# One end of a fused attention and expert layer: pad transfers asked for earlier, one weight copy given to a transfer, router and ranks one step forward

## What is computed

```
x  = x + tanh(g_attn) * attention(layernorm(x), ctx)      # causal, 16 heads, keys and values from ctx
y  = layernorm(x)
e  = argmax(softmax(y @ Wr + br))                          # one expert per token
out = sum over all experts i of  relu((y if e == i else 0) @ W1[i] + b1[i]) @ W2[i] + b2[i]
x  = x + tanh(g_ffn) * out
```

## Time and profile before

| what | value |
|---|---|
| time of the profiled execution | 349.75 us |
| its span (first to last instruction) | 347.8 us, 1.95 us less |
| median of 3 runs | 350.26 us, 0.51 us above the profiled one |
| PE busy | 335.7 us, 97% of the span |
| DVE, ACT, POOL busy | 285.8 us, 247.9 us, 197.5 us |
| TensorE clock granted | 0.997 of full speed |
| last batch begins | about 261.8 us |
| first expert tile | 294.3 us |
| tile 7 transposed | 310.25 us |
| last product ends | 341.8 us |

### The profile page before, as it was taken

One profiled execution on the slowest core, in us unless ns is written; L12 is line 12 of the kernel. 1 busy time (PEld: TensorE's weight loads), 2 busy tenths in 40 slices (PEclk: granted clock), 3 DMA queues, 4 the chain that ended last, 5 costly groups with the idle time before them and its releaser, 6 DMA issues.

```text
span 347.8 us, 10938 instructions
## 1 busy us (share of the span) xinstructions
PE 335.7 (97%) x2827; PEld 282.3 (81%) x2827; DVE 285.8 (82%) x1288; ACT 247.9 (71%) x908; POOL 197.5 (57%) x401
## 2 busy tenths in 40 slices
PE   7999999999999999999999999999999999989993
PEld 6777878887987788879887988798888767979992
DVE  4778997798889888898889878988998896877871
ACT  3687776588758875887588758876887666757671
POOL 7243755367636763766376637653867553157553
PEclk9999999999999999999999999999999999999998
DMA  6999022000300030003000300040001944434320
GB/s 201 249 357 296 7 94 96 4 2 1 126 0 0 0 125 0 0 0 125 0 0 0 125 0 0 0 140 0 0 0 76 401 180 129 125 97 116 115 67 13
DMA packets 22618, 28.39 MB, mean 82 GB/s; under 512 B 3681, under 2 KB 17845, under 8 KB 22592
## 3 DMA queue, kind: packets, MB, share of 16 engines
q1 hardware_dynamic: 20832, 24.37, 22.1%
q0 software_dynamic: 1504, 3.16, 2.5%
q10 hardware_dynamic: 256, 0.56, 0.6%
HBM read 19.52 MB, written 9.01 MB: 82 GB/s over the span
## 4 chain that ended last, share of the span: by engine, by line
PE 83%; DMA 4%; DVE 4%; issue 3%; SPq 3%; POOL 1%; POOLq 0%; DVEq 0%; ACT 0%
PE ps_kv L1402 20%; PE ps_o L1402 15%; PE ps_t L1532 12%; PE ps_w L1402 10%; PE ps_s L1402 10%; PE ps_q L1402 9%; PE ps_t L1402 6%; SPq L357 2%; DMA sorted_rows<-pad_rows 1%; DMA nat<-in_ctx 1%; SPq L358 1%; DMA sorted_rows<-rows,slot_i 1%; DVE prob_T L946 1%; DMA tile_in<-sorted_rows 1%; PE ps_s L1652 1%
## 5 line engine op out<-in xcount | busy, mean ns | idle before, releaser
L446 POOL TENSOR_SCALAR prob<-prob,row_inv 128x128 f32<-128x128 f32 (+1 forms) x256 | 107.8, 441 | 105.2 <-DVE row_inv L940 104.4
L601 ACT ACTIVATE prob<-prob,neg_max 128x128 f32<-128x128 f32 (+1 forms) x256 | 113.0, 450 | 19.1 <-DVE neg_max L900 19.0
L946 DVE COPY prob_T<-ps_t 128x384 f32<-128x384 f32 x123 | 63.1, 549 | 4.6 <-PE ps_t L1532 4.6
L900 DVE CUSTOM_DVE_ANT_0 prob<-ps_s,mask_now 128x128 f32<-128x128 f32 x206 | 57.4, 337 | 0.4 <-PE ps_s L1402 0.4
L1532 PE MATMUL ps_t<-ident,prob 128*128 128x128 f32 x384 | 54.6, 277 | 1.3 <-POOL prob L446 1.0
L1532 PEld LDWEIGHTS ps_t<-ident,prob 128*128 128x128 f32 x384 | 43.3, 141 | 14.1 <-issue 9.2
L601 ACT ACTIVATION_READ_ACCUMULATOR prob<-prob,neg_max 128x1 f32 x256 | 50.1, 196 | 0.0
L1402 PE MATMUL ps_o<-prob_T,v_nat 128*64 128x256 f32 (+1 forms) x512 | 49.8, 333 | 0.2 <-issue 0.2
L1402 PEld LDWEIGHTS ps_o<-prob_T,v_nat 128*64 128x64 f32 x512 | 31.8, 136 | 13.4 <-issue 2.6
L1402 PE MATMUL ps_s<-k_T,q_T 64*128 64x128 f32 (+1 forms) x412 | 41.7, 331 | 0.4 <-DVE q_T L1282 0.3
L542 POOL DMA_INDIRECT out<-tile_out,tile_in x23 | 23.4, 1018 | 26.1 <-DVE tile_out L1350 18.9
(11 more groups left out here) (205 smaller groups left out, 623.2 us busy)
## 6 DMA issues: line engine op xcount, KB each, us to landing
ctx_buf<-in_ctx SPq DMA_DIRECT2D x8, 768.0 KB
sorted_rows<-pad_rows SPq DMA_DIRECT2D x8, 642.5 KB, 4.5
tile_in<-sorted_rows SPq DMA_DIRECT2D x24, 128.5 KB, 2.2
packs<-in_L_ffn_W SPq DMA_DIRECT2D x1, 2048.0 KB
packs<-in_L_ffn_W SPq DMA_DIRECT2D x8, 256.0 KB
nat<-in_ctx SPq DMA_DIRECT2D x8, 128.0 KB, 3.5
nat<-in_x SPq DMA_DIRECT2D x1, 768.0 KB, 6.7
w_in<-in_L_xattn_Wk SPq DMA_DIRECT2D x2, 256.0 KB, 4.0
```

Source lines behind the costliest of these rows:

```text
L446: g.tensor_scalar(prob[:, slot, lo:hi], prob[:, slot, lo:hi], row_inv[:, slot, t:t + 1], 1.0, ALU.mult, ALU.mult).then_inc(prob_ready, 1)
L601: s.activation(prob[:, slot, lo:hi], prob[:, slot, lo:hi], ACT.Exp, bias=neg_max[:, slot, t:t + 1], scale=-1.0, accum_out=row_sum[:, slot, ...
L900: v.tensor_tensor_reduce(out=prob[:, slot, lo:hi], in0=scores, in1=mask_now[:, lo:hi], scale=-SCALE, scalar=FLOOR, op0=ALU.add, op1=ALU.mi ...
L946: v.tensor_copy(prob_T[:, slot % TSLOTS, :], ps_t[slot % 2][:, 0:W3]).then_inc(probT_kept, 1)
```

## The change

Five edits. (1) `pad_at` is written before the first maxima of the last batch and not after its first sums. (2) COPIED goes from 5 to 4: DVE makes four copies of second weights, and SP three transfers in place of two. (3) The router of batch 7 is issued before the last of the four products of `second_product(1)` and not behind it. (4) The ranks of batch 7 are issued ahead of `second_product(2)` and not in its middle. (5) On DVE, `place(7)` comes ahead of `early_rest(1)` and `finish(1, 1)`, a register load of tile 5's expert ahead of that, and `early_rest(5)` with a register load comes behind the weights of tile 7.

```
@@ sync
-            for i in range(2):
+            for i in range(EARLY - COPIED):
                 tile = COPIED + i
                 e = sp.value_load(tile_expert[0:1, tile:tile + 1], min_val=0, max_val=E - 1)
@@ vector, between
-                if here == 0:
-                    n.wait()
-                    v.tensor_copy(pad_at[:, :], next_row[0:1, :]).then_inc(pad_ready, 1)
@@ vector, batch
                     if last and j == 0:
+                        n.wait()
+                        v.tensor_copy(pad_at[:, :], next_row[0:1, :]).then_inc(pad_ready, 1)
                         shared_maxima(p + SUMS, SUMS)
@@ vector, end
             finish(0, 0)
             for step in range(6):
                 choose(B - 1, step)
+            experts[COPIED + 1] = expert_of(COPIED + 1)
+            for step in range(4):
+                place(B - 1, step)
             early_rest(1)
             finish(1, 1)
-            for step in range(4):
-                place(B - 1, step)
             early_rest(2)
             finish(2, 2)
...
             early_rest(4)
             finish(4, 4)
-            early_rest(5)
-            experts[COPIED + 1] = expert_of(COPIED + 1)
             expert = expert_of(EARLY)
             weights_of(EARLY, EARLY, 0)
             weights_of(EARLY, EARLY, 1)
+            early_rest(5)
+            experts[COPIED + 2] = expert_of(COPIED + 2)
             early_rest(6)
@@ tensor, end
-            def second_product(tile, r, between=None):
+            def second_product(tile, r, between=None, at=FC // 2):
                 wait(pe, out_ready, tile - 1)
                 for c in range(FC):
-                    if between and c == FC // 2:
+                    if between and c == at:
                         between()
...
-                second_product(tile - 1, tile - 1, ranks_of_last if tile == LN_AT + 1 else None)
-                if tile == LN_AT:
-                    router(B - 1)
+                if tile == LN_AT + 1:
+                    ranks(B - 1)
+                second_product(tile - 1, tile - 1, router_of_last if tile == LN_AT else None, FC - 1)
@@ tables
-EARLY_W2 = (34, 38, 39, 40, 41)
+EARLY_W2 = (34, 38, 39, 40)
-COPIED = EARLY - 2
+COPIED = EARLY - 3
```

More of the change, by code:

```diff
@@ L300, in flamingo_layer @@
         w1_early = sem("w1_early")
-        w2_loaded = [sem(f"w2_loaded{i}") for i in range(2)]
+        w2_loaded = [sem(f"w2_loaded{i}") for i in range(EARLY - COPIED)]
         w1_ready, w2_ready, h_done, h_kept = sem("w1_ready"), sem("w2_ready"), sem("h_done"), sem("h_kept")
@@ L1826, in second_product, with router_of_last @@
                 last.then_inc(y2_done, 1)
-            def ranks_of_last():
-                ranks(B - 1)
+            def router_of_last():
+                router(B - 1)
             def eighth_tile():
@@ L1848, in _ @@
                     pe.wait_ge(w2_loaded[tile - 1 - COPIED], 16)
-                second_product(tile - 1, tile - 1, ranks_of_last if tile == LN_AT + 1 else None)
-                if tile == LN_AT:
-                    router(B - 1)
-            pe.wait_ge(w2_loaded[1], 16)
+                if tile == LN_AT + 1:
+                    ranks(B - 1)
+                second_product(tile - 1, tile - 1, router_of_last if tile == LN_AT else None, FC - 1)
+            pe.wait_ge(w2_loaded[EARLY - 1 - COPIED], 16)
             second_product(EARLY - 1, EARLY - 1, eighth_tile)
@@ L1857, in _ @@
                     tile_transpose(tile + 1, (tile + 1) % RING)
-                    pe.wait_ge(w2_ready, tile - 2)
+                    pe.wait_ge(w2_ready, tile - (EARLY - COPIED))
                     second_product(tile - 1, (tile - 1) % RING)
-            pe.wait_ge(w2_ready, MT - 2)
+            pe.wait_ge(w2_ready, MT - (EARLY - COPIED))
             second_product(MT - 1, (MT - 1) % RING)
```

## The result

| kernel | median | lowest to highest | runs |
|---|---|---|---|
| before | 349.55 us | 348.67 to 350.86 | 14 |
| with the change | 350.61 us | 350.19 to 351.87 | 14 |

The ratio is 1.003 (95% interval 1.0018 to 1.0041): **slower by 0.3%**, 1.06 us. The forecast was 0.2 us faster, "the same".

The account below looks back on a forecast made before the run. PE, 83% of the last-ending chain, was taken as the bound, with tile 7's transpose deciding the end. Terms -0.3 + 0.1 = -0.2 took 349.75 to 349.55 us; the median, standing 0.51 above, gave 350.1, range 348.9 to 351.4.

Parts of the forecast that it names:

- the size of one landing: Batch 5's second scatter beside the early pads: lands after 3.9 us (bounds 2.6 to 4.8), DVE's `rows` waits 0.6 us.
- the slack of 0.6 to 0.7 us: Between DVE's copies and PE's transposes at 269.67: absorbs DVE's scatter wait, so 0.6 costs 0 and 1.5 costs 0.8 us.
- Edit 1's gain at the end: Earlier pads start POOL's batch 6 scatter 1.4 us earlier, but PE then waits before the last pair's values: worth 0.
- That row is not fed by POOL: DVE's unbroken instruction row for the early table, 278 to 289.4 us, would not shorten when POOL is earlier.
- DVE's row gets shorter: Rival, chance 0.17: tiny DVE instructions between 286 and 289.4 lose their excess, 1.0 us gained, 349.0 us.
- the stalls only move: Rival, chance 0.15: POOL's earlier scaling falls on DVE's last table steps; one 0.33 us excess cancels the gain, 350.3 us.
- stuck behind the pads: Rival, chance 0.13: scatter waits for whole pad transfers, 2.2 us each; net 0.7 slower behind one, 2.9 behind two; priced 352.1 us.
- Edit 2, 0.2 us at `rows`: One DVE copy fewer before batch 7's `rows`, which starts at 294.15 and not 294.36; the third SP transfer costs 0.
- Edits 3 to 5: Earlier router, ranks and places in batch 7: `logits` 0.4 us earlier including edit 2, `slot_i` and last scatter 0.65 us earlier.
- The late table: On DVE after `slot_i`: 0.37 us gained ahead, a register load of 0.4 to 0.45 added; starts at 303.9, before 303.86.
- Tile 7, 0.3 us earlier: SP issues tile 7's load at 307.75, not 308.05; its transpose comes at 309.95, not 310.25, leaving 0.3 of 0.65 us.
- Behind 310.25 PE runs without a gap: From tile 7's transpose PE runs unbroken to its last product, so when tile 7 is transposed decides the end.

Follow-up runs that it names:

- two pads ahead: Two pad transfers issued before batch 5's second scatter; forced on chip C by SP reading two places before issuing, against the kernel before: 351.24 us, 1.0046.
- the second buffer: The change plus a second rows buffer for batch 6, so `rows` waits for no scatter; against the kernel before: 0.9989 (A), 0.9987 (chip C), 0.9983 (D).
- chip C: Third group of four kernels, run beside the kernel before (349.72 us); the change itself took 351.44 us there, 1.0044.
- one pad ahead: One pad transfer issued before batch 5's second scatter, seen in traces of the change on chip B (0.9983) and edit 1 alone on A (0.9994).
- one pad went out and none followed: The change, with SP waiting for both scatters of batch 5 after the first pad transfer, against the kernel before on chip B: 0.9994.
- D: Fourth group, beside the kernel before (350.2 us): edits 2 to 5 1.0001, edit 1 alone 1.0066, edits 3 to 5 1.001, the second buffer 0.9983.
- A: First group, beside the kernel before (352.55 us): edits 2 to 5 1.0007, edit 1 alone 0.9994, SP waiting for scatters before pads 0.9998, the second buffer 0.9989.
- chip B: Second group, beside the kernel before (352.78 us): the change 0.9983, edits 2 to 5 1.0009, exactly one pad ahead of the scatters 0.9994, edits 3 to 5 1.0018.

## Why the prediction was wrong

**Edit 1 decided, and the step that failed is the size of one landing.** "I take 3.9 us, a landing at 267.3 and a wait of 0.6", with an upper bound of 4.8 us, "nearer to the disturbed rows, though the scatter meets the first pads and not a load in full flow". Measured were 5.6 to 5.8 us and a wait of 2.3 to 2.5 in the four profiles with one buffer and two pads ahead, above my upper bound; and 4.1 us and a wait of 0.83 and 0.90 where one was, near what I took. The bound was the longest landing of a row beside *one* transfer of 768 KB. In the changed kernel SP has eight to issue and nothing to wait for, and how many get ahead of the scatter was never counted. It could have been: `pad_at` at 261.7, SP's issues a little over 1 us apart, the scatter issued at 263.41 with an instruction of 0.96 us, and 17.3 us for eight transfers.

**A second term of that step failed: the slack of 0.6 to 0.7 us.** As a statement on PE's first gap it held behind two pads: 2.40 gave 1.71, 2.35 gave 1.65, 2.30 gave 1.62. Behind one pad it did not: 0.83 gave 0.41 and 0.90 gave 0.39, where 0.13 and 0.2 were due. And as the cost it is wrong: "a wait of 0.6 costs 0, one of 1.5 costs 0.8" took PE's gap for the whole, but DVE carries its own wait to the empties' product and to `slot_i` of batch 6 in full (2.35 us of wait, 2.24 there). That the loss is not made up behind it is as said: with two ahead, the first expert tile stands at 33.88 behind the projection, with the second buffer at 31.65, and that is 2.23.

**Edit 1's gain at the end, "worth 0": wrong by 0.53 us.** The waits before the last pairs' transposes shrank to 0.35 (I had said that none is left), and 0.69 appears before the last pair's values, both as I had argued. But "That row is not fed by POOL" missed that the row itself gets shorter once POOL's scatter does not wait, by 0.27 us, and what stands behind it by 0.26. This is the rival *DVE's row gets shorter*, which had a chance of 0.17 at 1.0 us: it came true at about half of its size, hidden under the loss. The 1x8 subtraction of 0.48 us took 0.15 in the profile of the change, while the `tile_expert` instruction 0.75 us behind it took 0.45 and the next 0.38, so a part of *the stalls only move* is seen too. Why these small instructions are longer or shorter was not tried.

**So two errors cancel.** With two pads ahead, my own rule would give 1.65 for the wait and 0 for the gain; measured are 2.2 and 0.53, 1.7 net, against 1.5 to 1.7 us in the times of chip C. That the sum fits is luck. It shows apart only where one of the two is missing: with the second buffer the cost is gone and the gain left (0.9987 and 0.9983, 0.5 us below before), and with one pad ahead the 0.9 us of cost and the 0.5 of gain leave too little to be told.

**The rival "stuck behind the pads" was what happened**, at a chance of 0.13. Its point of decision fits: the landing at 268.08 is 269.04 on the time axis of before, past 268.8. Its unit was wrong, 2.2 us a transfer, since I divided 17.3 us by eight and so counted SP's start and the last one's landing as well; a pad at 403 to 411 GB/s takes 1.6. On the rival's own sum that gives a wait of 1.1 us for one whole transfer and of 2.7 for two; measured were 0.83 and 0.90, and 2.30 to 2.53, and only 0.25 where one pad went out and none followed. The rule quoted from the Trainium skill, "DMA: Bandwidth & Descriptors", section on queues, rings and completion order, that a DMA engine alternates between its queues by whole packets, had made me keep this rival small; on these traces q0 moved 3 packets while q1 moved 220. The measurement decides: the scatter's packets were served behind the pads that were there first. Whether something ahead of the DMA engines held them back was not tried.

**Edit 2, 0.2 us at `rows`**: right in sign, 0.1 to 0.2 in size. With early pads `rows` stands 11.40 to 11.42 us behind `slot_i` of batch 6 with it (11.58 in one profile) and 11.50 without; with late pads 11.87 to 12.16 and 12.03 to 12.28. No line shows a wait for the third transfer.

**Edits 3 to 5** were to bring `logits` to 0.2 us nearer to `rows`, and `slot_i` 0.25 us nearer to `logits`; in the three profiles it is 0.10 to 0.12 and 0.14 to 0.16. **The late table** "still near 303.9" was to come 0.04 us later; it comes 0.26 to 0.55 later: less is gained ahead of it, and from `slot_i` to it are 1.57 us (1.5 in the forecast), where two more tile instructions stand. **Tile 7, 0.3 us earlier**, is the term that fails with it: 0.34 earlier in one profile, 0.03 earlier and 0.08 later in the others. Even the 0.34 us was gone two tiles on: "Behind 310.25 PE runs without a gap" was true of before, but a tile that comes earlier meets SP's next loads, which come every 1.3 us from the late table on. Together edits 2 to 5 were forecast at -0.3 us and measured at 1.0007, 1.0009 and 1.0001, zero within the interval.

**What beats both kernels** is the change with a second buffer and `early_rest(1)` in DVE's idle time ahead of the logits: 348.70 us against 349.72, 0.9964. With the buffer, the early pads cost nothing and their 0.53 us stay; with the moved instruction, the late table starts at 41.94 and no longer at 42.44 to 42.66, and tile 7 at 47.68. On that chip the buffer alone gives 349.18 us and the moved instruction 0.48 us more.

## What to carry to other kernels

- Before you start a long row of transfers earlier, count how many can be issued before each small transfer that something waits for, and price that one at the sum of those ahead of it (here about 1.4 us each, from landings of 2.8, 4.1 and 5.6 us with none, one and two ahead). A bound taken from a row with one large transfer beside it is no bound for two.
- If a small transfer must run beside large ones, free its source (a second buffer) rather than try to time it: with the buffer the landing was just as late, and cost nothing.
- A wait of one engine costs what that engine brings late further on, not only what another engine stands still at once. Compare positions well behind it: here 1.65 us of idle time of PE were 2.24 us at the end of DVE's row.
- A net time that fits can hold two errors. A kernel that takes away the cost and leaves the gain (the second buffer) tells them apart.
- When a wait is shortened on a path, follow the next two or three items of the engine that feeds it. Here SP's loads, 1.3 us apart, took back 0.34 us within two tiles.

## What was not expected of the hardware

**One program, two timings by the chip.** With one source, SP's second pad was issued 1.1 to 1.2 us behind the first in the profiles of the first result and of chips C and D (263.2 and 264.4 on C), and 1.5 us behind it on A and B (262.5 and 264.0); the records of these two issues last 362 and 333 ns on C and 16 and 13 ns on B. The scatter's instruction ends in between, and the change costs 1.5 to 1.7 us (ratio 1.0044) on chip C and nothing that can be told on chip B. Why SP differs is open, and also how often the second pad is in time on one chip: that was seen only in the profiled executions. It may be why the first result lost 1.06 us and not the 1.5 to 1.7 of chip C.

**The clock after a stall.** PE stood still for 1.6 to 1.8 us in four profiles with two pads ahead. In one of them (the first) the granted clock fell to 1.2 GHz behind the stall; in the other three it stayed at 1.00, as in this window of the change on chip C:

```profile
272.00:274.00 2.00, 2.00 (x15) 1.75 (x14) 1.79 (x12) 0.00 (x0) 0.35 (x2) 1.00 1.02 414
```

The lower clock cost PE 1.44 us in that stretch (5.70 against 4.26), of which 1.1 were left at the first expert tile (34.95 against 33.86 behind the projection). It accounts for most of the 1.26 us by which that one execution (351.87 us) lies above the median, and not for the median. What set it off there and not elsewhere was not found.
